# Latent queries of an attention layer by seven block products instead of eight, on one core of a Trainium2 chip

## The chip, the cores and the metric

The kernel runs on 1 core of one Trainium2 chip. The metric is the device time of one execution in microseconds, the median of the runs. Lower is better.

## The reference, cut to what matters

One layer over 2048 tokens of width 512: a layer norm, latent attention with 16 heads under a causal mask, a mixture of eight 512x512 factors, and the residual.

```python
xn = layernorm(x)                                   # x: 2048 x 512
q = (xn @ wq).reshape(s, 16, 192)                   # 128 plain + 64 rotary columns a head
ckv, k_pe = split(xn @ wkv_a, 128)                  # latent keys/values, rotary keys
ckv = ckv * rsqrt(mean(ckv**2) + 1e-6) * kv_norm_scale
k_nope, v = split((ckv @ wkv_b) per head, 128)
scores = (q_nope @ k_nope.T + rope(q_pe) @ rope(k_pe).T) * 192**-0.5, causal
out = x + (softmax(scores) @ v, heads joined) @ wo + mix(xn, factors) / sqrt(8) + bias
```

## The kernel before, in words

The keys of a head are never formed. The kernel multiplies a head's `wq` with its key part of `wkv_b` (the tile `wA`, 512 x 128), so that the product of the tokens with `wA` is a query in the latent space, and that query meets the latent keys `kTh`, `kTl` of all heads alike. Every float32 matrix is held as a high and a low float16 part, and every product is three matmuls (high*high, high*low, low*high: the helper `three`, L426 to L428).

The queries are taken in four passes of 512 tokens, `ORDER = (3, 2, 1, 0)`: pass one holds the last 512 tokens, which see all 2048 keys, pass four the first 512, which see 512 keys. A pass has 16 units, one for each head, so `NU = 64` units i. A unit has four rows r of 128 queries. In pass one a row of scores comes in four pieces of up to 512 keys, in pass two in three, in pass three in two, in pass four in one.

TensorE's program (`scores`, then `fills`, for each i and r) is written out in one order: the score matmuls of row (i, r) and, behind them, the list that `fills(i, r)` gives. Every engine walks the same lists for its own part of the work, strictly in its order, and semaphores tie them. In rows of passes two to four the list holds:

- `q`, in row 0: the latent query of the next unit, 4 k-slices x 3 = 12 matmuls of 512 columns (`q_latent`, L535). ScalarE copies it to the high part (L795), VectorE makes the low part (L1151). `wA` comes from DRAM, one head at a time.
- `out`, in each row: three matmuls that take head i-2's values (`oT`) through `wV`. The first of them waits for `v_o`, VectorE's low part of `oT` (L1212). VectorE makes it in row 0 of the same unit, behind that row's maxima (L1174, L1176, `rm` L1186, `nm` L1193). VectorE then adds each `out` to `acc` (L1227).
- `pv`: the values of head i-1, 16, 12, 8 or 4 key tiles in all, in rows 1 to 3 (pass two), 2 and 3 (pass three) or row 3 (pass four). Behind it ScalarE copies the result to `oT` (L829).
- `pe`, in row 3 of even units: the rotary queries of the next two heads, 12 matmuls.

For a row ScalarE takes the exponentials piece by piece (`ex`, L812) once VectorE has `nm`, and writes their high part (`st`, L822). GpSimd writes the low part (L1408), a DMA transposes both. In rows of passes three and four ScalarE does its part of `fills` behind all exponentials and high parts of the row.

## Time and profile before

| | |
|---|---|
| median of 3 runs | 1498.38 us (1497.08 to 1500.48) |
| span of the profiled execution, first to last instruction | 1496.9 us |
| granted TensorE clock, mean | 1.000 |
| TensorE matmuls | 1469.3 us busy, 98% of the span, 7908 instructions |
| chain that ended last | PE 92% |

The profiled execution has no time of its own beside its span, only the three unprofiled runs: their median is 1.4 us above the span. A matmul's duration in the rows is from its start to the last result; the next one starts well before that, so the distance of two starts is what a matmul costs TensorE.

### The profile page before, as it was taken

The numbers are of one execution on the slowest core, as the hardware profiler recorded it, in microseconds if no ns is written. First come the engines' busy times: TensorE is split into PE (matmuls) and PEld (weight loads), VectorE is DVE, ScalarE is ACT, GpSimd is POOL, SyncE is SP. The second block draws the span as 40 slices with busy tenths as digits, with TensorE's granted clock in tenths as the row PEclk, the third lists the DMA queues.
The fourth block names the chain that finished last, engine by engine and source line by source line (L and its number), as shares of the span: only waits on it lengthen the run. The fifth ranks groups of instructions, "written<-read, shape, count | busy, mean of one in ns | idle before, by whom it ended". The sixth has DMA issues, their size and how long they took to land.

```text
span 1496.9 us, 25751 instructions
## 1 busy us (share of the span) xinstructions
PE 1469.3 (98%) x7908; PEld 755.5 (50%) x7908; DVE 1014.5 (68%) x2563; ACT 965.7 (65%) x2404; POOL 911.3 (61%) x919
## 2 busy tenths in 40 slices
PE   6999999999999999999999999999999999999998
PEld 5544555555555545445444444445545555555554
DVE  7877677877777766656556565556666666676777
ACT  7877767677876567566566666665546665654554
POOL 3688777776665456575465656566645655664553
PEclk9999999999999999999999999999999999999999
DMA  6599999988777597787577677886856677754564
GB/s 202 152 199 203 211 193 186 191 163 158 157 157 132 127 193 149 140 178 139 118 145 141 137 133 145 173 151 130 162 112 136 137 139 152 156 141 95 115 132 110
DMA packets 646615, 227.84 MB, mean 152 GB/s; under 512 B 599376, under 2 KB 612176, under 8 KB 646096
## 3 DMA queue, kind: packets, MB, share of 16 engines
q1 hardware_dynamic: 646480, 226.20, 74.2%
q8 instruction: 65, 1.06, 0.3%
q14 instruction: 70, 0.57, 0.1%
HBM read 65.67 MB, written 17.83 MB: 56 GB/s over the span
## 4 chain that ended last, share of the span: by engine, by line
PE 92%; POOL 2%; DVE 2%; ACT 2%; DMA 1%; issue 1%; SPq 0%; POOLq 0%; DVEq 0%; ACTq 0%
PE ps L426 18%; PE ps L428 18%; PE ps L427 18%; PE ps L577 7%; PE ps L582 7%; PE ps L583 7%; PE ps L578 7%; PE ps L579 7%; POOL st L1408 2%; ACT ex L812 1%; DMA acc<-x_in 0%; DVE stats L944 0%; PE ps L450 0%; DVE acc L1227 0%; DMA pT<-st 0%
## 5 line engine op out<-in xcount | busy, mean ns | idle before, releaser
L1408 POOL TENSOR_TENSOR st<-ex,st 128x512 f16<-128x512 f32 (+3 forms) x640 | 637.8, 1015 | 488.9 <-ACT st L822 478.8
L812 ACT ACTIVATE ex<-ps,nm,scales 128x512 f32<-128x512 f32 (+3 forms) x640 | 452.0, 709 | 456.3 <-DVE nm L1193 439.8
L1174 DVE TENSOR_REDUCE gm<-ps 128x1 f32<-128x512 f32 (+1 forms) x384 | 249.0, 669 | 170.0 <-PE ps L583 166.0
L822 ACT ACTIVATE st<-ex 128x512 f16<-128x512 f32 (+3 forms) x640 | 343.0, 562 | 6.1 <-ACT ex L812 0.4
L577 PE MATMUL ps<-kTh,q 128*128 128x512 f16 (+3 forms) x640 | 222.3, 347 | 4.5 <-ACT ex L812 2.1
L426 PE MATMUL ps<-pT,vH 128*128 128x512 f16 (+3 forms) x640 | 222.1, 347 | 2.9 <-DMA pT<-st 2.9
L582 PE MATMUL ps<-kRh,q 128*128 128x512 f16 (+3 forms) x640 | 222.2, 347 | 0.0
L583 PE MATMUL ps<-kRl,q 128*128 128x512 f16 (+3 forms) x640 | 222.1, 347 | 0.0
L579 PE MATMUL ps<-kTh,q 128*128 128x512 f16 (+3 forms) x640 | 222.1, 347 | 0.0
L578 PE MATMUL ps<-kTl,q 128*128 128x512 f16 (+3 forms) x640 | 222.1, 347 | 0.0
L427 PE MATMUL ps<-pT,vH 128*128 128x512 f16 (+3 forms) x640 | 222.1, 347 | 0.0
L428 PE MATMUL ps<-pT,vL 128*128 128x512 f16 (+3 forms) x640 | 218.8, 347 | 0.0
L1227 DVE SCALAR_TENSOR_TENSOR acc<-ps,rden,acc 128x512 f32<-128x512 f32 x256 | 189.2, 743 | 3.5 <-PE ps L428 3.1
L1392 POOL TENSOR_TENSOR q<-rot,q 32x512 f16<-32x512 f32 x128 | 147.6, 1153 | 24.4 <-ACT q L801 11.6
L1176 DVE CUSTOM_DVE_ANT_0 ps<-ps,cmask 128x256 f32<-128x256 f32 (+3 forms) x256 | 133.0, 520 | 24.5 <-PE ps L583 21.8
L812 ACT ACTIVATION_READ_ACCUMULATOR ex<-ps,nm,scales 128x1 f32 x640 | 125.7, 196 | 0.0
L1151 DVE SCALAR_TENSOR_TENSOR q<-ps,q 128x512 f16<-128x512 f32 x64 | 44.2, 690 | 111.4 <-ACT q L795 111.4
L577 PEld LDWEIGHTS ps<-kTh,q 128*128 128x128 f16 x640 | 62.6, 98 | 72.8 <-ACT ex L812 9.5
L426 PE MATMUL ps<-wV,oT 128*128 128x512 f16 x256 | 97.0, 379 | 1.8 <-issue 1.5
L426 PE MATMUL ps<-xT,wA 128*128 128x512 f16 x256 | 97.0, 379 | 0.0
L427 PE MATMUL ps<-xT,wA 128*128 128x512 f16 x256 | 97.0, 379 | 0.0
L428 PE MATMUL ps<-xT,wA 128*128 128x512 f16 x256 | 97.0, 379 | 0.0
...
## 6 DMA issues: line engine op xcount, KB each, us to landing
...
```

Of the source, the lines that this page charges most:

```text
L426: e.matmul(o, a[0], b[0], start=first, stop=False)
L427: e.matmul(o, a[0], b[1], start=False, stop=False)
L428: return e.matmul(o, a[1], b[0], start=False, stop=last)
L577: e.matmul(b, q[:, i % 2, 0, qs], kTh[:, ks], start=True, stop=False)
L578: e.matmul(b, q[:, i % 2, 0, qs], kTl[:, ks], start=False, stop=False)
L579: e.matmul(b, q[:, i % 2, 1, qs], kTh[:, ks], start=False, stop=False)
L582: e.matmul(b, q[:, i % 2, 2, qs], kRh[:, ks], start=False, stop=False)
L583: e.matmul(b, q[:, i % 2, 2, qs], kRl[:, ks], start=False, stop=True).then_inc(z["p_s"], 1)
L812: e.activation(ex[:, n % NEX, 0:keys], s_bank(n)[:, 0:keys], ACT.Exp, bias=nm[:, (i * QT + r) % 4:(i * QT + r) % 4 + 1], scale=scales[:, p ...
L822: e.activation(stage(n, keys)[:, :, 0, :], ex[:, n % NEX, 0:keys].rearrange("p (t n) -> p t n", n=P), ACT.Copy).then_inc(z["a_pH"], 1)
L1174: e.tensor_reduce(m, b, AX_X, ALU.max).then_inc(z["v_max"], 1)
L1408: e.tensor_tensor(s[:, :, 1, :], ex[:, n % NEX, 0:keys].rearrange("p (t n) -> p t n", n=P), s[:, :, 0, :], ALU.subtract).then_inc(z["g_pL" ...
```

## The change

From pass two on, two heads 2g and 2g+1 are taken as one product: 512 x 256 weights by 512 x 512 tokens. It is cut in two by two blocks in each direction and done by Strassen's method in Winograd's form: seven block products `m1` to `m7` in place of eight. A block product is 2 k-slices x 3 matmuls of 256 columns. The blocks of weights and the four sums of them lie in `wS` (14 slots of 128 x 256), the four sums of token blocks in tiles that are free by then. The results are

- `c11 = m1 + m2` (head 2g, tokens 0 to 255), `c12 = m1 + m6 + m5 + m3` (head 2g, tokens 256 to 511),
- `c21 = m1 + m6 + m7 + m4` and `c22 = m1 + m6 + m5 + m7` (the same halves of head 2g+1).

`m1`, `m6`, `m5`, `m3` accumulate one on another in one PSUM bank; between them ScalarE copies the running sum out (`snapshot`, L1015) and TensorE waits for each copy. VectorE adds `m2`, `m7` and `m4` to these copies (`blocks_sum`, L1433). The high parts are ScalarE's (`block_high`), the low ones GpSimd's, but `c12`'s, which is VectorE's (`block_low`, L1438). In odd units TensorE does `m1` and `m2` in row 0, `m6` in row 1, `m5` in row 2, `m3` in row 3, in the even unit behind it `m7` in row 0 and `m4` in row 1. Unit 15 is the first with `m1`, unit 62 the last with `m7` (24 pairs in all).

In pass one the sums of weights are made, pair by pair: two copies of `wabs`'s bank and four high parts on ScalarE, two sums and four low parts on VectorE, two sums on GpSimd (`fills` "wabs", "sum", "sum_hi", "sum_lo"), and stored. GpSimd sums the blocks of tokens in nine steps a pass, in three units of the pass before. Loads of weights are 896 KB a pair instead of 512 KB. `XS` is halved and `BACK` doubled. Semaphores that only VectorE itself waits for are joined in one.

The core of the diff:

```diff
-XS, VS, KS, WS, PS, BACK = 2.0 ** 10, 2.0 ** 12, 2.0 ** 8, 2.0 ** 15, 2.0 ** 15, 2.0 ** -14
+XS, VS, KS, WS, PS, BACK = 2.0 ** 9, 2.0 ** 12, 2.0 ** 8, 2.0 ** 15, 2.0 ** 15, 2.0 ** -13
...
+HC = CH // 2
+A11, A12, S2, S1, S4, S3, A22 = range(7)
+G0 = H // 2
+TOKENS_HIGH = ((1, 2), (2, 3), (3, 6), (4, 7))
...
+STEPS = {"p_m": ("m1", "m2", "m6", "m5", "m3", "m7", "m4"), "a_m": ("m1", "c11", "m6", "m5", "c12", "c22", "c21"),
+         "v_m": ("c11", "c12", "c22", "c21"), "g_m": ("c11", "c22", "c21")}
...
+def done(engine, step, g):
+    return len(STEPS[engine]) * (g - H // 2) + STEPS[engine].index(step) + 1
...
+def token_slots(k):
+    return [(H - 3 + (n + 1) // QT, (n + 1) % QT) if k == 1 else ((k - 1) * H + 6 + n // 2, n % 2 * 2) for n in range(9)]
...
+    if r == 1:
+        if H <= i + 1 < NU and i % 2:
+            out += [("c11", (i + 1) // 2), ("m6", (i + 1) // 2)]
+        if H <= i < NU and i % 2 == 0:
+            out += [("c22", i // 2), ("m4", i // 2)]
+    if r == 2:
+        if H <= i + 1 < NU and i % 2:
+            out.append(("m5", (i + 1) // 2))
+        if H <= i < NU and i % 2 == 0:
+            out.append(("c21", i // 2))
     if r == 0:
-        if 1 <= i < NU - 1:
+        if 1 <= i < H - 1:
             out.append(("q", i + 1))
+        if H <= i + 1 < NU and i % 2:
+            out.append(("m1", (i + 1) // 2))
+        if H <= i < NU and i % 2 == 0:
+            out.append(("m7", i // 2))
         if 1 <= i <= H:
             out.append(("nv", i - 1))
         if i == SQUARED + 1:
...
             out.append(("parts", i + 1))
+    if r == 0 and H <= i + 1 < NU and i % 2:
+        out.append(("m2", (i + 1) // 2))
...
+    if r == 3 and H <= i + 1 < NU and i % 2:
+        out.append(("m3", (i + 1) // 2))
+    for m in range(G0):
+        if r == 3 and i == sum_slot(m):
+            out.append(("sum", m))
+        if r == 0 and i == sum_slot(m) + 1:
+            out.append(("sum_hi", m))
+        if r == 1 and i == sum_slot(m) + 1:
+            out.append(("sum_lo", m))
+    for k in range(1, NC):
+        if (i, r) in token_slots(k):
+            out.append(("tok", (k, token_slots(k).index((i, r)))))
     return out
...
+            def blocks(kind, o, w, b, first):
+                for n in range(2):
+                    ins = three(o[:, 0:HC], [weight_block(w, a)[:, n * P:(n + 1) * P] for a in range(2)],
+                                [b[a][:, n, :] for a in range(2)], first and n == 0, n == 1, kind not in ("m1", "m2", "m7"))
+                ins.then_inc(z["p_m"], 1)
...
+            def q_blocks(kind, g):
+                n, k = g - G0 + 1, g // G0
+                if kind == "m1":
+                    o = free_bank(("m1", g))
+                    e.wait_ge(z["d_lA"], 16 * n)
+                    if g % G0 == 0:
+                        e.wait_ge(z["d_xT"], 32 * k)
+                    blocks("m1", o, A11, [token_block(k, a, 0, 0) for a in range(2)], True)
+                elif kind == "m2":
+                    o = free_bank(("m2", g))
+                    blocks("m2", o, A12, [token_block(k, a, 1, 0) for a in range(2)], True)
+                elif kind == "m6":
+                    e.wait_ge(z["a_m"], done("a_m", "m1", g))
+                    e.wait_ge(z["d_lS"], 16 * n)
+                    if g % G0 == 0:
+                        e.wait_ge(z["g_tok"], 4 * k - 2)
+                    blocks("m6", bank(("m1", g)), S2, [summed(k, 2, a) for a in range(2)], False)
+                elif kind == "m5":
+                    e.wait_ge(z["a_m"], done("a_m", "m6", g))
+                    blocks("m5", bank(("m1", g)), S1, [summed(k, 1, a) for a in range(2)], False)
+                elif kind == "m3":
+                    e.wait_ge(z["a_m"], done("a_m", "m5", g))
+                    blocks("m3", bank(("m1", g)), S4, [token_block(k, a, 1, 1) for a in range(2)], False)
+                elif kind == "m7":
+                    o = free_bank(("m7", g))
+                    e.wait_ge(z["d_lB"], 16 * n)
+                    if g % G0 == 0:
+                        e.wait_ge(z["g_tok"], 4 * k - 1)
+                    blocks("m7", o, S3, [summed(k, 3, a) for a in range(2)], True)
+                elif kind == "m4":
+                    e.wait_ge(z["v_m"], done("v_m", "c22", g))
+                    if g % G0 == 0:
+                        e.wait_ge(z["g_tok"], 4 * k)
+                    blocks("m4", bank(("m7", g)), A22, [summed(k, 4, a) for a in range(2)], False)
...
-                if r == 0 and p == 0:
+                if r == 0 and p == 0 and i < H:
                     e.wait_ge(z["v_q"], i + 1)
+                if r % 2 == 0 and p == 0 and i >= H:
+                    engine, part = (("g_m", "c22" if r else "c21") if i % 2 else ("v_m", "c12") if r else ("g_m", "c11"))
+                    e.wait_ge(z[engine], done(engine, part, i // 2))
                 e.matmul(b, q[:, i % 2, 0, qs], kTh[:, ks], start=True, stop=False)
...
+            def weights_sums(h):
...
+                e.activation(weights_f(m, h % 2), bank(("wabs", h)), ACT.Copy, scale=1.0 / WS).then_inc(z["a_wf"], 1)
...
+            def snapshot(kind, g):
+                n = g - G0 + 1
+                e.wait_ge(z["p_m"], done("p_m", kind, g))
+                if n > 1:
+                    e.wait_ge(z["g_m"], done("g_m", {"m1": "c11", "m6": "c21", "m5": "c22"}[kind], g - 1))
+                else:
+                    e.wait_ge(z["v_sum"], 6 * G0)
+                e.activation(snap[kind], bank(("m1", g))[:, 0:HC], ACT.Copy, scale=BACK).then_inc(z["a_m"], 1)
+            def block_high(kind, g):
+                i = 2 * g
+                if kind == "c12":
+                    e.wait_ge(z["p_m"], done("p_m", "m3", g))
+                    e.activation(q_half(i, 0, 1), bank(("m1", g))[:, 0:HC], ACT.Copy, scale=BACK).then_inc(z["a_m"], 1)
+                    return
+                at, i, half = {"c11": ("m1", i, 0), "c22": ("m5", i + 1, 1), "c21": ("m6", i + 1, 0)}[kind]
+                e.wait_ge(z["v_m"], done("v_m", kind, g))
+                e.activation(q_half(i, 0, half), snap[at], ACT.Copy).then_inc(z["a_m"], 1)
...
+            def weight_sums(m):
...
+                e.wait_ge(z["a_wf"], 2 * m + 2)
+                e.tensor_tensor(f1[:, HC:CH], f1[:, 0:HC], f1[:, HC:CH], ALU.add).then_inc(z["v_sum"], 1)
+                e.wait_ge(z["v_sum"], 6 * m + 1)
+                e.tensor_tensor(f1[:, 0:HC], f0[:, 0:HC], f1[:, 0:HC], ALU.subtract).then_inc(z["v_sum"], 1)
...
+            def sums_low(m):
...
+                for n, (at, f) in enumerate(((S3, f1[:, 0:HC]), (S1, f1[:, HC:CH]), (S2, f0[:, 0:HC]), (S4, f0[:, HC:CH]))):
+                    e.wait_ge(z["a_sum"], 4 * m + n + 1)
+                    e.tensor_tensor(weight_block(at, 1), f, weight_block(at, 0), ALU.subtract).then_inc(z["v_sum"], 1)
...
+            def blocks_sum(kind, g):
+                use, at = {"m2": ("m2", "m1"), "m7": ("m7", "m5"), "m4": ("m7", "m6")}[kind]
+                e.wait_ge(z["a_m"], done("a_m", at, g))
+                e.wait_ge(z["p_m"], done("p_m", kind, g))
+                e.scalar_tensor_tensor(out=snap[at], in0=bank((use, g))[:, 0:HC], scalar=BACK, in1=snap[at],
+                                       op0=ALU.mult, op1=ALU.add).then_inc(z["v_m"], 1)
+            def block_low(g):
+                e.wait_ge(z["a_m"], done("a_m", "c12", g))
+                e.scalar_tensor_tensor(out=q_half(2 * g, 1, 1), in0=bank(("m1", g))[:, 0:HC], scalar=BACK,
+                                       in1=q_half(2 * g, 0, 1), op0=ALU.mult, op1=ALU.subtract).then_inc(z["v_m"], 1)
...
+            def block_low(kind, g):
+                i = 2 * g
+                at, i, half = {"c11": ("m1", i, 0), "c22": ("m5", i + 1, 1), "c21": ("m6", i + 1, 0)}[kind]
+                e.wait_ge(z["a_m"], done("a_m", kind, g))
+                e.tensor_tensor(q_half(i, 1, half), snap[at], q_half(i, 0, half), ALU.subtract).then_inc(z["g_m"], 1)
```

What stands in row 0 of unit 37 (pass three) on TensorE, before: the last six of the twelve matmuls of the latent query (`xT,wA`), and the first `out`.

```order
L426 MATMUL ps<-xT,wA 128x512
L427 MATMUL ps<-xT,wA 128x512
L428 MATMUL ps<-xT,wA 128x512
L426 MATMUL ps<-xT,wA 128x512
L427 MATMUL ps<-xT,wA 128x512
L428 MATMUL ps<-xT,wA 128x512
L426 MATMUL ps<-wV,oT 128x512 [waits s_d_lV1,s_v_o,s_v_ffn]
L427 MATMUL ps<-wV,oT 128x512
L428 MATMUL ps<-wV,oT 128x512
```

And now, from the last score matmul of that row on: `m1` (`xT,wS`), the same `out`, the start of `m2`.

```order
L759 MATMUL ps<-kRl,q 128x256
L557 MATMUL ps<-xT,wS 128x256 [waits s_d_lA,s_v_out]
L558 MATMUL ps<-xT,wS 128x256
L559 MATMUL ps<-xT,wS 128x256
L557 MATMUL ps<-xT,wS 128x256
L558 MATMUL ps<-xT,wS 128x256
L559 MATMUL ps<-xT,wS 128x256
L557 MATMUL ps<-wV,oT 128x512 [waits s_d_lV1,s_v_o,s_v_ffn]
L558 MATMUL ps<-wV,oT 128x512
L559 MATMUL ps<-wV,oT 128x512
L557 MATMUL ps<-xT,wS 128x256 [waits s_v_pe]
```

Six matmuls of 256 columns stand between the scores and the first `out` where twelve of 512 stood, and `out` waits for the same semaphore `v_o`.

VectorE, from the last `acc` of unit 37 through row 0 of unit 38, before (L1174 and L1176 are the maxima, L1212 the low part of `oT`, on which `v_o` stands, L1151 the low part of the query):

```order
L1227 SCALAR_TENSOR_TENSOR acc<-ps,rden,acc 128x512 [waits s_p_out,s_v_den,s_v_out]
L1174 TENSOR_REDUCE gm<-ps 128x1 [waits s_p_s]
L1176 ISA ps,gm<-ps,cmask 128x256 [waits s_p_s]
L1176 ISA gm 128x1
L1186 TENSOR_REDUCE rm<-gm 128x1 [waits s_v_max]
L1193 TENSOR_SCALAR nm<-rm,scales,head 128x1 [waits s_a_exp,s_v_rm]
L1212 SCALAR_TENSOR_TENSOR oT<-ps,oT 128x512 [waits s_a_o]
L1151 SCALAR_TENSOR_TENSOR q<-ps,q 128x512 [waits s_a_q]
L1227 SCALAR_TENSOR_TENSOR acc<-ps,rden,acc 128x512 [waits s_p_out,s_v_den,s_v_out]
```

And now (L1461 and L1463 are the maxima, L1499 the low part of `oT`, L1438 `c12`'s low part, L1433 `m7`'s sum):

```order
L1514 SCALAR_TENSOR_TENSOR acc<-ps,rden,acc 128x512 [waits s_v_den,s_p_out,s_v_out,s_v_ffn]
L1438 SCALAR_TENSOR_TENSOR q<-ps,q 128x256 [waits s_a_m]
L1461 TENSOR_REDUCE gm<-ps 128x1 [waits s_p_s]
L1463 ISA ps,gm<-ps,cmask 128x256 [waits s_p_s]
L1463 ISA gm 128x1
L1473 TENSOR_REDUCE rm<-gm 128x1 [waits s_v_max]
L1480 TENSOR_SCALAR nm<-rm,scales,head 128x1 [waits s_a_exp,s_v_rm]
L1499 SCALAR_TENSOR_TENSOR oT<-ps,oT 128x512 [waits s_a_o]
L1433 SCALAR_TENSOR_TENSOR wf<-ps,wf 128x256 [waits s_p_m,s_a_m]
L1514 SCALAR_TENSOR_TENSOR acc<-ps,rden,acc 128x512 [waits s_p_out,s_v_den,s_v_out]
```

`c12`'s low part, which waits for ScalarE, now stands ahead of unit 38's maxima and of `oT`. On ScalarE, its high part (L1022) stands behind row 3's high parts of the exponentials and the copy of `oT`. Before:

```order
L822 ACTIVATE st<-ex 128x4x128 [waits s_a_exp,s_d_pT6]
L822 ACTIVATE st<-ex 128x4x128 [waits s_a_exp,s_d_pT7]
L829 ACTIVATE oT<-ps 128x512 [waits s_p_out,s_p_pv]
L812 ACTIVATE ex,ssum<-ps,nm,scales 128x384 [waits s_g_pL,s_v_den,s_v_nm]
L812 ACTIVATE ex,ssum<-ps,nm,scales 128x256 [waits s_g_pL]
```

Now:

```order
L1053 ACTIVATE st<-ex 128x4x128 [waits s_a_exp,s_d_pT6]
L1053 ACTIVATE st<-ex 128x4x128 [waits s_a_exp,s_d_pT7]
L1060 ACTIVATE oT<-ps 128x512 [waits s_p_out,s_p_pv]
L1022 ACTIVATE q<-ps 128x256 [waits s_p_m]
L1043 ACTIVATE ex,ssum<-ps,nm,scales 128x384 [waits s_g_pL,s_v_den,s_v_nm]
```

ScalarE in row 1 of unit 37, before (exponentials and high parts, the rotary parts, the first exponential of row 2):

```order
L812 ACTIVATE ex,ssum<-ps,nm,scales 128x512 [waits s_g_pL,s_v_nm]
L812 ACTIVATE ex,ssum<-ps,nm,scales 128x256 [waits s_g_pL]
L822 ACTIVATE st<-ex 128x4x128 [waits s_a_exp,s_d_pT2]
L822 ACTIVATE st<-ex 128x2x128 [waits s_a_exp,s_d_pT3]
L801 ACTIVATE q<-rot 128x512 [waits s_p_s,s_g_rot]
L812 ACTIVATE ex,ssum<-ps,nm,scales 128x512 [waits s_g_pL,s_v_nm]
```

And now, with `c11`'s high part (L1026) and the copy of `m6` (L1015), for which TensorE's `m5` in row 2 waits:

```order
L1043 ACTIVATE ex,ssum<-ps,nm,scales 128x512 [waits s_g_pL,s_v_nm]
L1043 ACTIVATE ex,ssum<-ps,nm,scales 128x256 [waits s_g_pL]
L1053 ACTIVATE st<-ex 128x4x128 [waits s_a_exp,s_d_pT2]
L1053 ACTIVATE st<-ex 128x2x128 [waits s_a_exp,s_d_pT3]
L1026 ACTIVATE q<-ktmp 128x256 [waits s_v_m]
L1015 ACTIVATE ktmp<-ps 128x256 [waits s_g_m,s_p_m]
L1032 ACTIVATE q<-rot 128x512 [waits s_p_s,s_g_rot]
L1043 ACTIVATE ex,ssum<-ps,nm,scales 128x512 [waits s_g_pL,s_v_nm]
```

The copy has come in behind the row's exponentials, high parts and `c11`.

## Rows read from the trace of the kernel before

**Rows 1.** The page: busy time of engines (share of span), granted clock in 40 slices.

```profile
PE 1469.3 (98%) x7908; PEld 755.5 (50%) x7908; DVE 1014.5 (68%) x2563; ACT 965.7 (65%) x2404; POOL 911.3 (61%) x919
...
PEclk9999999999999999999999999999999999999999
```

**Rows 2.** Groups by form, TensorE: count, busy us, mean ns, idle before.

```profile
L426 PE MATMUL ps<-xT,wA 128*128 128x512 f16 x256 | 97.0, 379 | 0.0
```

**Rows 3.** TensorE's waits: us in total, times, longest.

```profile
PE ps L500 <- ACT ex L686: 6.9, 1, 6.9
PE ps L426 <- DMA pT<-st: 2.9, 2, 1.8
```

**Rows 4.** Timeline, unit 21 (pass two), row 0: start, duration in us, engine, line.

```profile
736.37 0.27 PE L582 MATMUL ps<-kRh,q 128*128 128x256 f16 x1
...
736.48 0.27 PE L583 MATMUL ps<-kRl,q 128*128 128x256 f16 x1
...
736.59 0.38 PE L426 MATMUL ps<-xT,wA 128*128 128x512 f16 x1
...
736.81 0.38 PE L427 MATMUL ps<-xT,wA 128*128 128x512 f16 x1
...
736.84 0.43 DVE L1176 CUSTOM_DVE_ANT_0 ps<-ps,cmask 128x256 f32<-128x256 f32 x1
...
737.18 0.14 DVE L1176 DVE_READ_ACCUMULATOR2_ANT gm<- 128x1 f32 x1
...
737.36 0.16 DVE L1186 TENSOR_REDUCE rm<-gm 128x1 f32<-128x3 f32 x1
...
737.55 0.27 DVE L1193 TENSOR_SCALAR nm<-rm,scales,head 128x1 f32<-128x1 f32 x1
...
737.74 0.68 DVE L1212 SCALAR_TENSOR_TENSOR oT<-ps,oT 128x512 f16<-128x512 f32 x1
...
739.18 0.38 PE L426 MATMUL ps<-wV,oT 128*128 128x512 f16 x1
```

**Rows 5.** Timeline, unit 21 (pass two), row 3: last score matmul, ScalarE's `oT`.

```profile
755.00 0.38 PE L583 MATMUL ps<-kRl,q 128*128 128x512 f16 x1
...
760.55 0.59 ACT L829 ACTIVATE oT<-ps 128x512 f16<-128x512 f32 x1
```

**Rows 6.** Timeline, unit 37 (pass three), row 3, the same with the high parts.

```profile
1121.19 0.38 PE L583 MATMUL ps<-kRl,q 128*128 128x512 f16 x1
...
1124.42 1.14 ACT L822 ACTIVATE st<-ex 128x512 f16<-128x512 f32 x2
...
1125.46 0.59 ACT L829 ACTIVATE oT<-ps 128x512 f16<-128x512 f32 x1
```

**Rows 7.** Timeline, unit 37, row 1: last score matmul, ScalarE's exponentials, high part.

```profile
1113.36 0.27 PE L583 MATMUL ps<-kRl,q 128*128 128x256 f16 x1
...
1115.30 0.78 ACT L812 ACTIVATE ex<-ps,nm,scales 128x512 f32<-128x512 f32 x1 [2.91 <-DVE nm L1193]
...
1116.07 0.55 ACT L812 ACTIVATE ex<-ps,nm,scales 128x256 f32<-128x256 f32 x1
...
1116.61 0.62 ACT L822 ACTIVATE st<-ex 128x512 f16<-128x512 f32 x1
```

**Rows 8.** Timeline, pass four: row 3 of unit 55, row 0 of unit 56.

```profile
1398.32 0.38 PE L583 MATMUL ps<-kRl,q 128*128 128x512 f16 x1
...
1401.29 0.30 DVE L1176 CUSTOM_DVE_ANT_0 ps<-ps,cmask 128x128 f32<-128x128 f32 x1
...
1401.51 0.77 ACT L812 ACTIVATE ex<-ps,nm,scales 128x512 f32<-128x512 f32 x1
...
1401.88 0.68 DVE L1212 SCALAR_TENSOR_TENSOR oT<-ps,oT 128x512 f16<-128x512 f32 x1
...
1402.46 0.63 ACT L822 ACTIVATE st<-ex 128x512 f16<-128x512 f32 x1
...
1403.00 0.44 ACT L812 ACTIVATE ex<-ps,nm,scales 128x128 f32<-128x128 f32 x1
```

More of the change, by code:

```diff
@@ L1 @@
+import itertools
 from contextlib import ExitStack
@@ L232, in bank_order, with take @@
             pre.append(("q", 0))
-    body = [k for i in range(NU + 2) for r in range(QT) for k in fills(i, r) if k[0] in IN_BANKS or k == ("nrm", 2)]
-    return pre, body
+    bank, before, last, held = {}, {}, {}, {}
+    def take(key, b):
+        bank[key], before[key], last[b] = b, last.get(b), key
+    for n, key in enumerate(pre):
+        take(key, [MB, MB + 1, MB + 2, OB][n % 4])
+    free = [MB + n for n in range(MBANKS)]
+    for i in range(NU + 2):
+        for r in range(QT):
+            for key in fills(i, r):
+                if key[0] in IN_BANKS or key == ("nrm", 2):
+                    b = free.pop(0)
+                    take(key, b)
+                    if key[0] in LEFT:
+                        held[LEFT[key[0]], key[1]] = b
+                    else:
+                        free.append(b)
+                elif key in held:
+                    free.append(held.pop(key))
+    return pre, bank, before
 def build(nc, x, wq, wkv_a, wkv_b, wo, kvs, factors, bias, rope_t, rope_n, out):
@@ L424, in _, with three @@
         def _(e):
-            def three(o, a, b, first=True, last=True):
-                e.matmul(o, a[0], b[0], start=first, stop=False)
-                e.matmul(o, a[0], b[1], start=False, stop=False)
-                return e.matmul(o, a[1], b[0], start=False, stop=last)
+            def three(o, a, b, first=True, last=True, more=False):
+                e.matmul(o, a[0], b[0], start=first, stop=False, skip_group_check=more)
+                e.matmul(o, a[0], b[1], start=False, stop=False, skip_group_check=more)
+                return e.matmul(o, a[1], b[0], start=False, stop=last, skip_group_check=more)
             def count(key):
@@ new lines, in sums_high @@
+            def sums_high(m, which):
+                if which < 2:
+                    e.wait_ge(z["v_sum"], 6 * m + 2)
+                else:
+                    e.wait_ge(z["g_sum"], 2 * m + 2)
+                if m and which == 0:
+                    e.wait_ge(z["d_sS"], 16 * m)
+                f = weights_f(m, 1 if which < 2 else 0)
+                if which < 2:
+                    parts = ((S3, slice(0, HC)), (S1, slice(HC, CH)))
+                else:
+                    parts = ((S2, slice(0, HC)), (S4, slice(HC, CH)))
+                at, cols = parts[which % 2]
+                e.activation(weight_block(at, 0), f[:, cols], ACT.Copy).then_inc(z["a_sum"], 1)
@@ L833, in fill @@
                     q_latent(n)
+                elif kind == "wabs":
+                    weights_sums(n)
+                elif kind == "sum_hi":
+                    for which in range(4):
+                        sums_high(n, which)
+                elif kind == "tok":
+                    k, s = n
+                    for t, at in TOKENS_HIGH:
+                        if at == s:
+                            tokens_high(k, t)
+                elif kind == "m1":
+                    snapshot("m1", n)
+                elif kind == "m6":
+                    snapshot("m6", n)
+                elif kind == "m5":
+                    snapshot("m5", n)
+                elif kind == "m3":
+                    block_high("c12", n)
+                elif kind in ("c11", "c22", "c21"):
+                    block_high(kind, n)
                 elif kind == "parts":
@@ L937, in _, with own @@
         def _(e):
+            chained = itertools.count(1)
+            def own():
+                return next(chained)
             def norm_stats(p2):
@@ L1387, in rope_parts @@
                     e.wait_ge(z["g_pL"], piece(i - 1, r, chunk(i - 1)) + 1)
+                    if r == 1 and i >= H:
+                        e.wait_ge(z["g_m"], done("g_m", "c22" if i % 2 else "c11", i // 2))
                 hi = q[:, i % 2, 2, :]
```

310 lines of the change are left out of this document (235 added, 75 removed).

## The prediction

> **What bounds the kernel now.** I read the page first: TensorE is busy for 1469.3 of 1496.9 us, the other engines for 61% to 68% [rows 1]. Then its waits: the longest two sums are 6.9 us, one wait at the start, and 2.9 us [rows 3], so from the first scores to the tail nothing that another engine does is late for it. Then the timeline, where the distance of two starts is the cost of a matmul: 736.59 to 736.81, that is 0.216 us for 512 columns, and 736.37 to 736.48, 0.109 us for 256 [rows 4]. Half the columns cost half the time, so the kernel is bound by columns through TensorE, and the weight loads lie under them at 256 columns too. The question for the change is therefore double: how many columns go, and what was covered by them.
>
> **What goes.** A latent query is 12 matmuls of 512 columns (768 of the three lines in 64 units, a third of them in [rows 2]), 12 x 0.216 = 2.59 us, a pair of heads 5.18 us. Seven block products are 42 matmuls of 256 columns, 42 x 0.109 = 4.58 us, one of them 0.65 us. A pair gains 0.60 us, 24 pairs 14.3 us. The weight load keeps pace in the scores of 256 columns [rows 4], and I take 0.109 us as it is. With nothing late this alone would give 1484.
>
> **First wait: `out` in row 0.** In rows of passes two to four the first `out` needs `v_o`, the low part of `oT`, which VectorE makes only after that row's maxima. In unit 21 the scores of row 0 leave TensorE at 736.59. VectorE takes the last piece at 736.84, reads the accumulator, reduces, scales, and its `oT` runs from 737.74 to 738.42 [rows 4]. So `v_o` stands 1.83 us behind the scores and cannot stand sooner: VectorE began 0.09 us after the last score had landed (736.48 + 0.27), and did nothing else in between. Before, the query's 2.59 us lay in this place and `out` came at 739.18 [rows 4], 0.76 us after `v_o`. Now `m1` (odd units) or `m7` (even units) lies there, 0.65 us, and `m2` stands behind `out`. With 0.03 us for the semaphore TensorE waits 1.83 + 0.03 - 0.65 = 1.2 us. What is queued behind it is all of TensorE's program. The same chain of instructions runs in every unit, so this is 1.2 us in each of 24 odd units: 29 us. Even units are worse:
>
> **Second wait: the same `out`, even units.** VectorE's last work of an odd unit is now `c12`'s low part, which waits for ScalarE's high part, and that stands behind row 3's exponentials, their high parts and the copy of `oT`. Unit 38's maxima and `oT` queue behind it. Prices for 256 columns, which the trace has in like form: on ScalarE 0.33 us to the next start and 0.44 us to the result (between 128 and 512 columns, whose exponential high parts take 0.54 us at most to the next start [rows 8]); on VectorE 0.34 us, as the maximum of 256 (736.84 to 737.18) [rows 4]. I count from the end T of row 3's scores.
>
> - Pass three, T = 1121.41. ScalarE starts `oT` at 1125.46 [rows 6], T + 4.05, is free at + 4.55 (0.50 later), `c12` is there at + 4.99. VectorE: low part to + 5.36, maxima of 384 and 256 (0.48 + 0.34), accumulator, `rm`, `nm` (0.18 + 0.19 + 0.19, [rows 4]) to + 6.74, `oT` to + 7.42. TensorE: `out` 0.65, `pv` 1.62, `m3` 0.65, scores 1.36, `m7` 0.65 = + 4.93. It waits 7.45 - 4.93 = 2.5 us.
> - Pass two, T = 755.22: `oT` at 760.55 [rows 5], + 5.33; `c12` at + 6.27; a third piece of maxima, 0.60, in front; `oT` ready at + 9.30. TensorE has 1.08 us more scores and comes at + 6.01: 3.3 us.
> - Pass four, T = 1398.54: here ScalarE copies `oT` before the exponential (1401.51), the high part follows at 1402.46 and it is free at 1403.00 [rows 8], + 4.46; `c12` at + 4.90; VectorE's low part to + 5.27, maximum of 128 to `oT` 0.59 (1401.29 to 1401.88) [rows 8], ready at + 6.57. TensorE comes at + 3.85: 2.7 us.
>
> Eight even units a pass: 8 x (3.3 + 2.5 + 2.7) = 68 us.
>
> **Third wait: `m5`.** `m6` waits for the copy of `m1`, which ScalarE makes about 3.9 us after row 0's scores in pass three; TensorE comes at 4.8 us, since it lost 1.2 before. No wait. `m5` needs the copy of `m6`, behind row 1's exponentials. Pass three, T = 1113.47: even with VectorE free at once `nm` ends at T + 1.24 (0.19 to start, 0.07 for the piece before, 0.98 of work), exponentials 0.77 (1115.30 to 1116.07) and 0.54 (to 1116.61) [rows 7], two high parts 0.52 + 0.33, `c11` 0.33, `m6` 0.44: + 4.24. TensorE has `m6`, `out` and 1.89 us of scores in front, 3.19: it waits 1.05 us, in 8 units. In pass four the same chain is 2.9 us (one piece, 0.74 for its exponential) against 0.65 + 0.65 + 0.81 = 2.1: 0.8 us in 7 units. In pass two four tiles of `pv` (2.59 us) lie in front too: none. Together 14 us.
>
> `m3` and `m4` I cost at nothing: `out` and `pv` (2.3 us) hide the copy of `m5`; `m7`'s sum follows `oT` on VectorE by 0.44 us, while TensorE has `out` and scores (1.2 us and more). If that cover went, 24 pairs would pay up to 0.5 us each.
>
> **Pass one, GpSimd, DMA.** The sums of a pair add some 3 us on ScalarE, 2 on VectorE and 1.4 on GpSimd in two units of pass one, which last 60 us and more; the nine steps of token sums add some 17 us of GpSimd to three units. All stand where these engines idle a third of the time, and pass one keeps its full query in row 0. I take nothing; lower bound 0, upper bound 5 us, if GpSimd's steps make the low parts late.
>
> **The sum.** - 14.3 + 29 + 68 + 14 = + 97 us on the profiled span of 1496.9: 1594. The runs' median is 1.4 us above that span: 1595.
>
> **A rule against the change.** The profile grants the full clock (2.4 GHz) in every slice, even the first, which holds the 6.9 us wait [rows 1, 3]. The Trainium skill ("TensorE: Matmul & The Clock Gate", HAM oscillation) says that pauses between bursts of matmuls can bring the clock back to its lower level. By the row these pauses cost themselves alone, + 97; by the rule each of the long ones might cost as long again in slow matmuls, which is rival D.
>
> **The rivals.**
>
> - A, the three waits as worked out: 1595, own range 1578 to 1612 (half a microsecond more or less in 48 units is 24, less what cancels). Chance 0.68.
> - B, only the first wait. If ScalarE or VectorE took `c12` early enough not to hold the next unit, even units would wait 1.2 us as well: - 14.3 + 24 x 1.2 x 2 + 14 = + 57, 1555. The order of the instructions speaks against it. Chance 0.12.
> - C, faster: `v_o` is no obstacle, since the waits of a unit sum to under 0.30 us, from where the columns decide. All 14.3 us would come: 1484. For it speaks only that TensorE never waited for `v_o` before; against it that the query which hid it is gone, and that 1.83 us of VectorE's chain cannot be shorter [rows 4]. Chance 0.06.
> - D, slower still: the clock falls to 1.2 GHz in the wake of the waits of 2.5 us and more. Where it does, matmuls cost twice; if 3 us of matmuls follow each of 24 such waits at that level, 1.5 to 3 us more each: 1631 to 1667. Against it stands the first slice [rows 1, 3]. Chance 0.09.
> - E, a stall that I did not see (a load of `wS` or a transpose behind it in SP's queue), over 20 us more: chance 0.05, 1620 to 1650.
>
> **How the numbers follow.** 1595 is A's. The range 1552 to 1625 holds A, B and part of E, some 0.82. No change from 1498.38 can be told below 0.2%, some 3 us; only C lies on the faster side, and hardly anything falls within: faster 0.06, same 0.01, slower 0.93.
>
> **What would show it.** In the profile after: TensorE's matmul count up by 432, its busy time 1455 to 1465 us (the ends of matmuls run on into each wait); TensorE's waits led by `wV,oT` matmuls released by VectorE's `oT`, some 97 us in 48 waits, longest about 3.3 in pass two, 1.2 in odd units; next the block products released by ScalarE's copies, 14 us. VectorE waiting about 24 times for ScalarE's `c12`. The prediction is wrong if the first `out` of a unit starts without idle time before it, if the gap in even units is that of odd ones (B), or if the clock row shows less than 9 (D).

## The result, and the profile after

| | before | after |
|---|---|---|
| median | 1498.99 us (1497.08 to 1500.48) | 1653.14 us (1652.31 to 1658.33) |
| ratio, 95% interval | | 1.104 (1.102 to 1.106), slower |
| span of the profiled execution | 1496.9 us | 1650.4 us |
| granted TensorE clock, mean | 1.000 | 0.974 |

The change costs 154 us. The direction was forecast; 1595 us with a range up to 1625 was not enough. The busy times of the changed kernel's engines, against [rows 1]:

```profile
PE 1504.4 (91%) x8340; PEld 804.3 (49%) x8340; DVE 1065.7 (65%) x2659; ACT 1015.6 (62%) x2584; POOL 1019.7 (62%) x1049
```

432 matmuls more, as counted; but the idle time, 27.6 us before (1496.9 - 1469.3), is 146.0 now (1650.4 - 1504.4), 118 us more, and the busy time rose by 35 us where the columns alone would have lowered it. Both have to be explained. TensorE's waits (us in total, times, longest), against [rows 3]:

```profile
PE ps L557 <- issue: 84.6, 46, 3.6
PE ps L753 <- ACT ex L1043: 17.5, 13, 3.3
PE ps L557 <- ACT ktmp L1015: 11.5, 15, 2.0
PE ps L634 <- ACT ex L864: 6.9, 1, 6.9
PE ps L608 <- DVE oT L1499: 5.0, 2, 4.0
PE ps L557 <- DVE wf L1433: 2.3, 1, 2.3
```

The first row is the first `out` of a unit. It carries "issue" since VectorE's `oT` had ended in the profile when the matmul got going; the timeline shows that it is what ended the wait. L608, a small product over the same values (`nv`), stands ahead of the first `out` in units 15 and 16 and waits for the same `oT`, 1.0 and 4.0 us; unit 62 has no `out` in row 0, and the 2.3 us fall on its `m4` (L1433). So these three waits belong to the forecast's first and second waits as well, 84.6 + 5.0 + 2.3 = 91.9 us in all:

```profile
621.34 0.58 PE L608 MATMUL ps<-nv,ones 128*128 128x2 f32 x2 [3.97 <-DVE oT L1499]
```

Four waits of TensorE, in passes two (odd, even), three and four, from there:

```profile
652.40 0.38 PE L557 MATMUL ps<-wV,oT 128*128 128x512 f16 x1 [1.12 <-issue]
...
679.72 0.59 PE L557 MATMUL ps<-wV,oT 128*128 128x512 f16 x1 [3.13 <-issue]
...
1115.81 0.39 PE L557 MATMUL ps<-wV,oT 128*128 128x512 f16 x1 [2.34 <-issue]
...
1445.83 0.38 PE L557 MATMUL ps<-wV,oT 128*128 128x512 f16 x1 [2.53 <-issue]
```

VectorE ahead of the second of them:

```profile
676.63 0.42 DVE L1438 SCALAR_TENSOR_TENSOR q<-ps,q 128x256 f16<-128x256 f32 x1 [4.12 <-ACT q L1022]
676.98 1.15 DVE L1461 TENSOR_REDUCE gm<-ps 128x1 f32<-128x512 f32 x2
678.04 0.42 DVE L1463 CUSTOM_DVE_ANT_0 ps<-ps,cmask 128x256 f32<-128x256 f32 x1
678.38 0.14 DVE L1463 DVE_READ_ACCUMULATOR2_ANT gm<- 128x1 f32 x1
678.55 0.16 DVE L1473 TENSOR_REDUCE rm<-gm 128x1 f32<-128x3 f32 x1
678.75 0.27 DVE L1480 TENSOR_SCALAR nm<-rm,scales,head 128x1 f32<-128x1 f32 x1
678.93 0.68 DVE L1499 SCALAR_TENSOR_TENSOR oT<-ps,oT 128x512 f16<-128x512 f32 x1
```

VectorE stands 4.12 us for ScalarE's high part of `c12`, with the maxima and `oT` queued behind it. That is the forecast's second wait as it was drawn. The matmul that it releases takes 0.59 us instead of 0.38: there the clock had fallen. The stretch behind it (start:end, length, then busy us and instructions of TensorE, weight loads, VectorE, ScalarE, GpSimd, then the granted clock, DMA share, GB/s) has half the full clock:

```profile
679.70:682.40 2.70, 2.68 (x7) 1.00 (x8) 1.00 (x2) 2.66 (x9) 1.23 (x2) 0.50 0.60 160
```

The four passes of the changed kernel (start:end, length, TensorE's busy us and matmuls, then the same three):

```profile
53.70:614.30 560.60, 538.78 (x2888) 1.00 0.84 170
614.30:1066.70 452.40, 417.20 (x2228) 0.97 0.67 138
1066.70:1412.60 345.90, 309.15 (x1712) 0.96 0.60 131
1412.60:1650.40 237.80, 200.02 (x1190) 0.94 0.45 109
```

A clock of 0.94 to 0.97 is a mean over stretches at 2.4 GHz and some at the lower level, 1.2 GHz; read in half microseconds, the clock falls 24 times in passes two to four. The page's row of slices, where a 9 stands for 90% or more, is still all nines for this kernel, so it can't show these falls. The passes before (length, then busy us of TensorE, weight loads, VectorE, ScalarE, GpSimd, then the clock):

```profile
54.00:596.00 542.00, 536.77 (x2870) 272.53 (x2871) 397.82 (x996) 390.05 (x980) 368.10 (x357) 1.00 0.85 169
596.00:1004.00 408.00, 408.00 (x2083) 201.49 (x2082) 240.78 (x568) 257.31 (x630) 246.42 (x237) 1.00 0.75 144
1004.00:1301.00 297.00, 296.77 (x1566) 150.81 (x1564) 191.10 (x492) 175.70 (x436) 174.29 (x174) 1.00 0.70 141
1301.00:1496.90 195.90, 188.72 (x1067) 97.67 (x1064) 144.03 (x373) 101.76 (x245) 101.37 (x108) 1.00 0.55 121
```

So pass one lost 19 us, the other three 44, 49 and 42.

Pass one, which the forecast took at nothing, shows most of its loss at one place, in row 2 of every second unit. VectorE of the changed kernel:

```profile
207.64 1.71 DVE L1427 TENSOR_TENSOR wS<-wf,wS 128x256 f16<-128x256 f32 x2
209.27 2.18 DVE L1427 TENSOR_TENSOR wS<-ktmp,wS 128x256 f16<-128x256 f32 x2
211.37 1.87 DVE L1461 TENSOR_REDUCE gm<-ps 128x1 f32<-128x512 f32 x3
```

and TensorE, 1.76 us late for the next row's scores, since their bank still waits for the exponential, and this for the maxima:

```profile
215.24 0.39 PE L753 MATMUL ps<-kTh,q 128*128 128x512 f16 x1 [1.76 <-ACT ex L1043]
```

The four low parts of a pair (L1427) were costed at 0.34 us each and take 0.86 and 1.09 here.

### The profile page after: what moved, and what is told of

Same layout as the page of the kernel before. It is cut to its first block, busy times and chain, and to the rows that moved or that the text cites. A ratio compares the mean times of both kernels' runs of the same rounds, so it can differ in the third digit from the quotient of the medians.

```text
span 1650.4 us, 27318 instructions
## 1 busy us (share of the span) xinstructions
PE 1504.4 (91%) x8340; PEld 804.3 (49%) x8340; DVE 1065.7 (65%) x2659; ACT 1015.6 (62%) x2584; POOL 1019.7 (62%) x1049
## 4 chain that ended last, share of the span: by engine, by line
PE 74%; DVE 9%; issue 9%; ACT 7%; DMA 1%; POOL 0%; ACTq 0%; DVEq 0%; SPq 0%; POOLq 0%
PE ps L557 15%; PE ps L559 14%; PE ps L558 14%; PE ps L753 6%; PE ps L754 6%; PE ps L755 6%; PE ps L758 6%; PE ps L759 6%; ACT ex L1043 4%; DVE gm L1461 2%; DVE wS L1427 2%; DVE ps L1463 1%; DVE nm L1480 1%; DVE acc L1514 1%; ACT st L1053 0%
## 5 line engine op out<-in xcount | busy, mean ns | idle before, releaser
L1461 DVE TENSOR_REDUCE gm<-ps 128x1 f32<-128x512 f32 (+1 forms) x384 | 249.4, 670 | 195.1 <-PE ps L759 192.0
L753 PE MATMUL ps<-kTh,q 128*128 128x512 f16 (+3 forms) x640 | 227.3, 355 | 19.9 <-ACT ex L1043 17.5
L1514 DVE SCALAR_TENSOR_TENSOR acc<-ps,rden,acc 128x512 f32<-128x512 f32 x256 | 190.2, 747 | 84.6 <-PE ps L559 83.3
L754 PE MATMUL ps<-kTl,q 128*128 128x512 f16 (+3 forms) x640 | 227.5, 356 | 0.0
L755 PE MATMUL ps<-kTh,q 128*128 128x512 f16 (+3 forms) x640 | 226.9, 355 | 0.0
L557 PE MATMUL ps<-pT,vH 128*128 128x512 f16 (+3 forms) x640 | 222.8, 348 | 2.2 <-DMA pT<-st 2.2
L557 PE MATMUL ps<-wV,oT 128*128 128x512 f16 x256 | 100.7, 393 | 84.9 <-issue 84.6
L1463 DVE CUSTOM_DVE_ANT_0 ps<-ps,cmask 128x256 f32<-128x256 f32 (+3 forms) x256 | 133.2, 520 | 26.7 <-PE ps L759 23.2
L753 PEld LDWEIGHTS ps<-kTh,q 128*128 128x128 f16 x640 | 63.8, 100 | 93.2 <-ACT ex L1043 31.1
L559 PE MATMUL ps<-wV,oT 128*128 128x512 f16 x256 | 102.1, 399 | 0.0
L558 PE MATMUL ps<-wV,oT 128*128 128x512 f16 x256 | 101.7, 397 | 0.0
L557 PEld LDWEIGHTS ps<-pT,vH 128*128 128x128 f16 x640 | 62.8, 98 | 66.2 <-issue 3.0
L558 PEld LDWEIGHTS ps<-pT,vH 128*128 128x128 f16 x640 | 62.7, 98 | 63.9 <-issue 0.8
```

Source lines behind the costliest of these rows:

```text
L557: e.matmul(o, a[0], b[0], start=first, stop=False, skip_group_check=more)
L558: e.matmul(o, a[0], b[1], start=False, stop=False, skip_group_check=more)
L559: return e.matmul(o, a[1], b[0], start=False, stop=last, skip_group_check=more)
L753: e.matmul(b, q[:, i % 2, 0, qs], kTh[:, ks], start=True, stop=False)
L754: e.matmul(b, q[:, i % 2, 0, qs], kTl[:, ks], start=False, stop=False)
L755: e.matmul(b, q[:, i % 2, 1, qs], kTh[:, ks], start=False, stop=False)
```

## The experiments

All are edits of the changed kernel (median 1653.1); the kernel before stood at 1498.4 to 1498.7 beside them.

**1. TensorE's waits filled with matmuls** (`wait_filled`), and **only the first part of the even ones** (`half_filled`). Matmuls of no use go into the empty bank, ahead of the wait for `v_o`; this is work added, with nothing changed in the output.

```diff
                 b = free_bank(("out", n))
+                if t == 0 and H <= i + 2 < NU - 2:
+                    u = i + 2
+                    for _ in range(((5, 5, 4) if u % 2 else (14, 10, 11))[u // H - 1]):
+                        e.matmul(b, kTh[:, 0:P], kTh[:, 0:CH], start=True, stop=True)
                 e.wait_ge(z["v_o"], i + 1)
```

> The changed kernel, with matmuls put into TensorE's waits for the values' output in row 0 of passes two to four: 5 in odd units (4 in pass four), 14, 10 and 11 in even ones, 512 columns each (0.21 us a matmul), into the bank that the first `out` then starts afresh. Nothing else moves; they end about when the wait would. Theory A (the lower clock comes from TensorE's long empty stretches): the granted clock stays at 1.00, the 43 us that the lower clock cost are back, 1653 - 43 = 1610 us (1600 to 1620). Theory B (the clock falls for another reason, such as the work around it): 1653 us within 8, mean granted clock still near 0.97.

> The changed kernel, with matmuls in the even units' waits for `out` alone, and only for their first part: 9, 6 and 7 of 512 columns in passes two, three and four instead of 14, 10 and 11, so that TensorE still stands for the last 1.0 to 1.3 us; the odd units' waits of 1.1 us stay empty. Theory A (only an empty stretch of more than 2 us lowers the clock): granted clock 0.99 or more, and the time is that of the filled waits, 1625 us (1620 to 1632). Theory B (every empty microsecond lowers it by its share): half of the lower clock stays, 1636 to 1645 us, mean clock near 0.985.

Measured: 1625.3 us (1624.4 to 1626.0) and 1625.0 (1622.3 to 1626.1), mean clock 0.996 and 0.994. Three stretches of 50 us of the changed kernel and then of the half-filled one (length, busy us and instructions of the five engines as above, clock, DMA share, GB/s):

```profile
650.00:700.00 50.00, 45.75 (x245) 23.75 (x244) 26.98 (x67) 29.34 (x75) 32.63 (x33) 0.97 0.76 159
...
1066.00:1116.00 50.00, 42.15 (x241) 23.17 (x240) 26.68 (x71) 27.49 (x71) 31.28 (x31) 0.97 0.61 135
1430.00:1480.00 50.00, 42.02 (x263) 24.73 (x262) 29.98 (x80) 22.92 (x60) 27.73 (x30) 0.93 0.45 118
```

```profile
650.00:700.00 50.00, 47.75 (x266) 25.41 (x265) 26.63 (x65) 31.21 (x80) 34.16 (x33) 1.00 0.75 155
1066.00:1116.00 50.00, 45.25 (x259) 24.84 (x260) 30.75 (x83) 27.35 (x72) 30.31 (x32) 1.00 0.70 142
1430.00:1480.00 50.00, 46.45 (x280) 25.78 (x278) 31.80 (x80) 21.22 (x56) 23.45 (x27) 1.00 0.40 98
```

The clock comes back and with it 28 us, by adding work to the engine that bounds the kernel. For the filled kernel theory A holds in kind, not in size: 28 us, not 43. The 43 were the missing 0.026 of the clock times 1650 us, as if TensorE lost half of every stretch at the lower level; where it was waiting for others anyway, it lost nothing (experiment 2 gives the price without added matmuls). By passes the filled kernel has 445.5, 332.4 and 228.2 us, that is 7, 14 and 10 us less; the matmuls put in, 81 us of them, take the place of 78 us of idle time, and four falls are left in each of the two kernels. The half-filled kernel still waits 49.0 us in these 46 places, 1.1 us each (one of them 2.3), and does as well, which is theory A of its forecast: the even units' long waits, 2.3 to 3.6 us, bring the clock down, and waits of 1.1 us do not. Length alone does not decide it, though. In the changed kernel one wait of 2.33 us (at 1208.67) has no slow matmul behind it, and in `out_later` (experiment 3) only 5 of 16 waits of 2.27 to 2.36 us do. What else decides is open.

**2. `c12`'s low part late** (`c12_late`).

```diff
-         "v_m": ("c11", "c12", "c22", "c21"), "g_m": ("c11", "c22", "c21")}
+         "v_m": ("c11", "c22", "c12", "c21"), "g_m": ("c11", "c22", "c21")}
...
         if H <= i < NU and i % 2 == 0:
-            out.append(("m7", i // 2))
+            out += [("m7", i // 2), ("c12", i // 2)]
...
-                elif kind == "m3":
+                elif kind == "c12":
                     block_low(n)
```

> The changed kernel, with VectorE's low part of `c12` moved from row 3 of the odd unit to row 0 of the even unit, behind the maxima and the sum of `m7` (scores of row 2 are the first to need it). Theory A (the maxima of row 0 stand behind this low part, and it behind ScalarE's copy and TensorE's `m3`, and this makes the even units' wait for `out` longer than the odd ones'): the even waits come down from 3.1, 2.3 and 2.5 us to 1.0 to 1.3, which gives 8 x (1.9 + 1.2 + 1.3) = 35 us, and with no wait over 1.3 us most of the 43 us of lower clock: 1653 - 75 = 1578 us (1565 to 1595). Theory B (ScalarE's copy of `c12` ahead of the values' read ends the wait): the even waits stay within 0.5 us of what they are, 1640 to 1653 us.

Measured: 1578.35 us (1577.8 to 1579.3), clock 0.998: theory A. Its waits for the first `out`, and its busy times:

```profile
PE ps L557 <- issue: 47.4, 46, 1.6
...
PE 1469.5 (93%) x8340; PEld 793.2 (50%) x8340; DVE 1067.2 (68%) x2659; ACT 1012.8 (64%) x2584; POOL 1017.6 (65%) x1049
```

1.03 us each in the mean, odd and even units nearly alike: this is the forecast's first wait alone. One instruction of 0.42 us, moved by one row, was worth 75 us, half of what the change had lost. The span is 73.5 us shorter, and it splits cleanly: TensorE's idle time falls from 146.0 to 107.4 us, 39 us, and its busy time, with the same 8340 matmuls, from 1504.4 to 1469.5, 35 us. The falls of the clock go from 25 to 2, so a fall cost some 1.5 us of TensorE's time. The expectation had 35 and 40 for the two; that their sum came out to the microsecond is luck.

**3. The first `out` in row 1** (`out_later`): `fills` gives rows 0 to 3 of units 16 to 61 the outputs (), (0, 1), (2,), (3,), and `ffn` and `store_output` the same places.

> The changed kernel, with the first `out` of each unit of passes two to four (and row 0's `ffn` product) moved from row 0 to row 1, behind `m6` or `m4` and ahead of that row's own `out`. Theory A (only the place of the first `out`, with no matmuls between the values and it, makes TensorE wait): some 80 us of waits go and with them the lower clock's 43: 1653 - 123 = 1530 us (1515 to 1550), the waits at `m6` and `m5` (some 18 us) stay. Theory B (VectorE and ScalarE are as late for the scores of row 1, whose banks the exponentials of row 0 must leave): the wait comes back at L753 in row 1 with half its length or more, 1580 to 1620 us.

Measured: 1591.5 us (1587.9 to 1592.4), clock 0.990: inside theory B's range, with B's mechanism in part. TensorE's waits (L757 and L561 are here what L753 and L557 are in the changed kernel):

```profile
PE ps L757 <- ACT ex L1047: 32.9, 19, 3.4
PE ps L561 <- DVE wf L1437: 27.5, 16, 2.4
PE ps L561 <- ACT ktmp L1019: 16.3, 29, 1.4
```

The odd units' waits are gone. The even units' come back, at the next thing that needs VectorE: in pass two at row 1's scores, as B had it (7 waits, 16.2 of the 32.9 us; the others are pass one's), in passes three and four at `m4`, which needs `m7`'s sum (L1437) and which neither theory named:

```profile
682.06 0.39 PE L757 MATMUL ps<-kTh,q 128*128 128x512 f16 x1 [2.31 <-ACT ex L1047]
...
1097.16 0.28 PE L561 MATMUL ps<-wsk,wS 128*128 128x256 f16 x1 [0.99 <-DVE wf L1437]
...
1459.18 0.28 PE L561 MATMUL ps<-sqr,wS 128*128 128x256 f16 x1 [2.27 <-DVE wf L1437]
```

So there are two causes: odd units have only too little work ahead of the first `out`; in even units VectorE itself is late, and moving TensorE's work does not help it.

**4. Pass one.** VectorE's four low parts shrunk to one column (`low_shrunk`), made by GpSimd (`low_gpsimd`), and spread over three rows (`low_spread`).

```diff
-                    e.tensor_tensor(weight_block(at, 1), f, weight_block(at, 0), ALU.subtract).then_inc(z["v_sum"], 1)
+                    e.tensor_tensor(weight_block(at, 1)[:, 0:1], f[:, 0:1], weight_block(at, 0)[:, 0:1], ALU.subtract).then_inc(z["v_sum"], 1)
```

> The changed kernel, with VectorE's four low parts of the weights' sums in pass one shrunk to one column each (the rest of the sums' low parts is left at zero by four memsets of GpSimd in the stage ahead of pass one: this part of the computation is left out). Theory A (the wait at L753 in pass one is the 3.9 us that these four take a pair): L753's waits for ScalarE in pass one fall from 16.7 us to some 2, 1653 - 17 = 1636 us (1631 to 1642). Theory B (ScalarE's four high parts and the copy to wf/kf are what makes the row late, or pass one's time is lost elsewhere): within 5 us of 1653.

> The changed kernel, with the four low parts of the weights' sums in pass one made by GpSimd instead of VectorE, in the same row 1 (all parts computed). VectorE's maxima of row 2 no longer stand behind 3.9 us a pair. Theory A (that delay of the maxima is what pass one lost, as the shrunk run showed with 12 us): L753's waits fall from 16.5 to 5 us, 1641 us (1637 to 1645). Theory B (GpSimd, at 1.05 us each by its own sums, makes its low parts of the exponentials late, whose buffers the exponentials wait for): no gain or a loss, 1650 to 1662 us. If both engines slow one another through their reads of SBUF, GpSimd's durations show it in either case.

> The changed kernel, with VectorE's four low parts in pass one spread over rows 1, 2 and 3 (two, one, one) in six of the eight pairs, instead of all four in row 1. Theory A (3.9 us at one place are more than a row can hide, 1 to 2 us are not): the waits at L753 fall to 5 to 8 us, 1644 us (1640 to 1647). Theory B (VectorE has no room anywhere in pass one, so each part delays the row it stands in): 1650 to 1656 us.

Measured: 1640.85 us (1638.6 to 1641.9), 1643.2 (1637.7 to 1647.3) and 1645.9 (1644.6 to 1647.4). L753's waits, in this order:

```profile
PE ps L753 <- ACT ex L1043: 5.4, 7, 1.6
```

```profile
PE ps L753 <- ACT ex L1043: 5.6, 8, 2.2
```

```profile
PE ps L754 <- ACT ex L1044: 8.4, 8, 3.2
```

These four instructions are 7 to 12 us of pass one's 19, and theory A holds in all three runs, though the shrunk one, at 1636 expected, kept 5 us more than I thought. Four runs of `low_gpsimd` spread over 10 us, so its order among the three is not certain. GpSimd takes 0.67 to 0.71 us for each, not the 1.05 of my expectation. Of what is left 7.8 us are four waits of 1.65 to 2.18 us in the first 180 us of pass one (in `low_gpsimd`). That the first pair's sums, which fall together with the start, make them is not shown.

**5. The price of a low part by itself** (`side_by_side`).

```diff
+                    ins = e.tensor_tensor(weight_block((S2, S1, S4, S3)[n % 4], 1), wf[:, n % 2 * HC:(n % 2 + 1) * HC],
+                                          weight_block((S2, S1, S4, S3)[n % 4], 0), ALU.subtract)
...
+                    ins = e.scalar_tensor_tensor(out=q_half(n % 2, 1, n // 2 % 2), in0=ps[:, MB, 0:HC], scalar=BACK,
+                                                 in1=q_half(n % 2, 0, n // 2 % 2), op0=ALU.mult, op1=ALU.subtract)
...
+                e.tensor_tensor(wA[:, n % 2, 0, :], ex[:, n % NEX, :], wA[:, n % 2, 1, :], ALU.subtract).then_inc(z["b_g"], 1)
```

> The changed kernel with a tail behind its last unit: VectorE makes 8 low parts as in pass one (128x256, f16 out of f32 and f16 in SBUF) and 8 low parts with their f32 operand in PSUM (as those of `c12`), first with GpSimd idle, then again while GpSimd runs 24 low parts of 128x512 out of SBUF (1.0 us each). The span grows by some 25 to 30 us. Theory A (two engines' reads of SBUF get in each other's way): VectorE's 8 of SBUF take 0.41 us with GpSimd idle and 0.9 to 1.4 us with it busy, those with PSUM stay within 0.1 us of one another. Theory B (the long ones in pass one are long for another reason, such as the transfers, at 85% there): 0.4 to 0.5 us in both halves.

Measured, VectorE and then GpSimd behind the last unit (one execution):

```profile
1650.86 2.88 DVE L1619 TENSOR_TENSOR wS<-wf,wS 128x256 f16<-128x256 f32 x8
1653.78 2.87 DVE L1627 SCALAR_TENSOR_TENSOR q<-ps,q 128x256 f16<-128x256 f32 x8
1657.91 10.40 DVE L1619 TENSOR_TENSOR wS<-wf,wS 128x256 f16<-128x256 f32 x8 [1.26 <-POOL wA L1872]
1668.34 2.87 DVE L1627 SCALAR_TENSOR_TENSOR q<-ps,q 128x256 f16<-128x256 f32 x8
```

```profile
1656.72 28.13 POOL L1872 TENSOR_TENSOR wA<-ex,wA 128x512 f16<-128x512 f32 x24 [18.91 <-DVE q L1627]
```

8 low parts out of SBUF take 2.88 us while GpSimd is idle, 10.40 us while it works; the same 8 with an operand in PSUM take 2.87 us either way. GpSimd's own instructions take 1.15 us alone and 1.33 (median of the first ten) beside VectorE's. Theory A had 0.9 to 1.4 us for VectorE's; only the span grew by 35 us and not by 25 to 30. VectorE gets in one instruction for each of GpSimd's: 1.30 us each. The Trainium skill ("SBUF — State Buffer", SBUF: two separate sides) says that a VectorE instruction with two SBUF inputs and a GpSimd one that reads SBUF exclude each other for their whole length. These rows agree: the two took turns, and the one with its operand in PSUM went by. The two kinds of low part are also different instructions (`tensor_tensor` and `scalar_tensor_tensor`); that it is the operand and not the instruction that counts, these rows alone don't show.

**6. All orders together** (`reordered`), and **with pass one's low parts on GpSimd** (`combined`). In rows 1 and 2 of passes two to four:

```
before: row 1: c11, m6 (or c22, m4), out 1;          row 2: m5 (or c21), out 2
now:    row 1: out 0, c11, m6 (or c22, m4), out 1;   row 2: out 2, m5 (or c21)
```

and in ScalarE's loop, for passes three and four:

```diff
+                    ahead = ("m1", "c11", "m6") if i < NU and last < 2 and r < 2 else ()
                     for kind, n in fills(i, r):
-                        if kind in late:
+                        if kind in late + ahead:
                             fill(kind, n)
```

> The changed kernel, with four orders changed together, nothing left out: `c12`'s low part late (as in c12_late), the first `out` of a unit in row 1 ahead of `m6` or `m4`, `m5` behind the `out` of row 2, and ScalarE's copies of `m1` and `m6` (and `c11`) ahead of the high parts in passes three and four. Theory A (the waits of passes two to four are only matters of order; the 16 us of pass one stay): from 1578 us the 47 us of waits for `out`, the 11 us at `m5` and about 0.17 us of start-up at each of some 60 waits go, less a few that come back: 1578 - 65 = 1513 us (1503 to 1523), clock at 1.00. Theory B (VectorE is late by itself in row 0, and the wait comes back at `m4` and the scores of row 1 as it did with the first `out` moved alone, 27 us): 1530 to 1555 us.

> The changed kernel with the orders of the run reordered and the low parts of pass one on GpSimd as in low_gpsimd; nothing left out. Theory A (the causes lie in different passes and add): 1520.5 - 10 = 1510.5 us (1506 to 1514), clock at 1.00, so the two kinds of causes explain 143 of the 154 us and the change without them is still no faster than the kernel before. Theory B (GpSimd, which has less room in passes without waits, or the new order makes the gains overlap): 1515 to 1521 us. A version that beats the kernel before would need under 1496 us.

Measured: 1520.5 us (1518.5 to 1522.5), then 1508.25 (1506.3 to 1509.4), both in theory A's range. The second is 1.0061 (1.0048 to 1.0075) of before; clock 0.999. The orders explain 145 of the 154 us, and the rest is no gain. The passes of the combined kernel, against those of before:

```profile
54.40:606.40 552.00, 539.82 (x2888) 274.85 (x2889) 414.91 (x1010) 410.41 (x1035) 416.25 (x420) 1.00 0.83 172
606.40:1014.10 407.70, 404.89 (x2228) 214.80 (x2226) 243.66 (x584) 267.67 (x674) 277.34 (x275) 1.00 0.76 153
1014.10:1310.10 296.00, 293.71 (x1713) 164.36 (x1712) 192.41 (x508) 186.33 (x482) 205.49 (x211) 1.00 0.71 152
1310.10:1506.80 196.70, 184.61 (x1190) 109.18 (x1187) 149.36 (x389) 105.22 (x279) 115.25 (x130) 1.00 0.59 133
```

TensorE is busy 3.1, 3.1 and 4.1 us less in passes two, three and four. That gain is real, but waits of 0.2 to 0.4 us, a 2.6 us one in the last two units and pass one's 10 us take more than it. No version faster than before was found; the start of pass one, where most of the last 10 us lie, was not tried.

## Why the prediction was wrong, point by point

- **What bounds the kernel, and what goes (- 14.3):** right in kind. Busy time falls by 10.3 us in passes two to four of the combined kernel. The profile counts as busy also the end of the matmul ahead of each wait: it is 0.38 us long, where the next start would be 0.216 us off, so 0.17 us a wait. The sum had no term for this.
- **First wait (29):** 1.12, 1.11 and 0.8 to 1.0 us in odd units: right.
- **Second wait (68):** 3.13, 2.33 and 2.53 us where 3.3, 2.5 and 2.7 were drawn: right, and for the reason given, as `c12_late` shows; rival B fell with it. First and second come to 91.9 us, with the waits at L608 and in unit 62, instead of 97.
- **Third wait (14):** 11.5 us, 0.79 each in pass three where 1.05 was forecast (the terms that the prediction lists there add to 4.17, not 4.24: 0.98).
- **`m3` and `m4` at nothing:** right as the kernel stands but for unit 62, and the cover is thin. With the first `out` moved, `m4` waited 27.5 us in all.
- **Pass one at nothing, at most 5:** this step failed. It lost 19 us. I had priced the sums by a maximum that reads PSUM (0.34), while their operands both lie in SBUF beside a busy GpSimd (0.86 and 1.09 in the rows above, 1.30 in the run by itself). And I had asked whether VectorE idles a third of the time, not whether the maxima of the next row stand right behind.
- **The clock at nothing (rival D, 0.09):** this step failed as well, and it is the largest. It cost 35 us of TensorE's time (`c12_late`), 28 us as the runs with the waits filled give it back. I weighed D by one row, the wait of 6.9 us in the first slice with the full clock, which comes once. In the changed kernel 24 long waits come one after another. D's price, 1.5 to 3 us a wait, was right at its lower end: 1.5 for each fall. That D's range, 1631 to 1667, holds the result is in part luck: at 1.5 us D gives 1631, and pass one's loss, which D did not have, makes up most of the rest. D's sign, a clock row under 9, was badly chosen: the row stayed at 9 in every slice, and only the mean (0.974) and short stretches show the falls. The Trainium skill's rule as the prediction gives it ("TensorE: Matmul & The Clock Gate", HAM oscillation) was the better guide here, and the trace agrees with it in kind: pauses between bursts of matmuls did bring the clock down. Waits of 2.3 to 3.1 us, shorter than the gaps that the page names, mostly did so, and waits of 1.1 us did not; where the two differ, these rows decide.

The sum in measured terms goes by TensorE's idle and busy time. Idle time rose by 118 us: the waits of passes two to four that were forecast are 103 of them (91.9 + 11.5), the waits for the exponential at L753, most of them in pass one, 15 (17.5 now, 2.1 before). Busy time rose by 35 us: the clock + 35, the columns - 14, and the ends of matmuls ahead of 69 more waits, at 0.17 us each, + 12 (an estimate). That is 151 of the 154 us. The forecast had + 111 for the waits and - 14 for the columns and stopped there: its waits came out 8 us shorter, and the clock, pass one and the ends of matmuls, which it had at nothing, 62 us longer.
